# Feed-forward attention: projected rows stay in PSUM through bias and rope; GpSimd makes the whole low part of the later weight pieces

## What is computed

```python
h = _rms_norm(x, ln1_w)                       # 256 selected rows, 512 wide
q = (h @ wq + bq).reshape(S, N_HEADS, HEAD_DIM)      # 16 heads of 128
kk = (h @ wk + bk).reshape(S, N_KV_HEADS, HEAD_DIM)  # 8
v = (h @ wv + bv).reshape(S, N_KV_HEADS, HEAD_DIM)
q = q * cos + _rotate_half(q) * sin
kk = kk * cos + _rotate_half(kk) * sin
...
att = jnp.einsum('shd,thd->hst', q, kk) / np.sqrt(HEAD_DIM)   # causal, softmax
attn_out = jnp.einsum('hst,thd->shd', att, v).reshape(S, N_HEADS * HEAD_DIM) @ wo
x1 = x + attn_out
mlp = jax.nn.silu(h2 @ w_gate) * (h2 @ w_up) @ w_down
```

## Time and profile before

| | us |
|---|---|
| median of 3 timed runs | 909.02 (906.36 to 913.1) |
| span of the profiled execution | 901.1 |
| TensorE busy in it | 826.7 |
| VectorE busy | 622.7 |
| ScalarE busy | 474.8 |
| GpSimd busy | 453.8 |

### The profile page before, as it was taken

One profiled execution on the slowest core, in us unless ns is written; L12 is line 12 of the kernel. 1 busy time (PEld: TensorE's weight loads), 2 busy tenths in 40 slices (PEclk: granted clock), 3 DMA queues, 4 the chain that ended last, 5 costly groups with the idle time before them and its releaser, 6 DMA issues. The chain is left out here.

```text
span 901.1 us, 14347 instructions
## 1 busy us (share of the span) xinstructions
PE 826.7 (92%) x4216; PEld 688.0 (76%) x4216; DVE 622.7 (69%) x1053; ACT 474.8 (53%) x1620; POOL 453.8 (50%) x501
## 2 busy tenths in 40 slices
PE   6999958999999999999999999999977677767997
PEld 5888747888888888888888888888755566656886
DVE  4454445777778777777777777777767988873932
ACT  4556435665565656655655665566552434443441
POOL 2333343555564565555565555565574664442660
PEclk9999989999999999999999999999998988999999
DMA  6656553111111111111112112110156342213520
GB/s 202 205 188 219 176 177 129 26 58 58 35 47 58 35 47 58 35 47 58 45 37 70 35 35 70 47 44 27 45 171 224 133 148 73 85 47 117 187 94 23
DMA packets 49288, 81.38 MB, mean 90 GB/s; under 512 B 4144, under 2 KB 12464, under 8 KB 49264
## 3 DMA queue, kind: packets, MB, share of 16 engines
q1 hardware_dynamic: 48688, 79.25, 26.9%
q0 software_dynamic: 576, 1.84, 0.6%
HBM read 63.77 MB, written 17.30 MB: 90 GB/s over the span
## 5 line engine op out<-in xcount | busy, mean ns | idle before, releaser
L1026 ACT ACTIVATE sq_junk<-q_row 128x128 bf16<-128x128 f32 x256 | 76.1, 298 | 157.6 <-DVE q_row L1280 157.6
L1034 ACT ACTIVATE p_row<-s_row,neg_max 128x128 f32<-128x128 f32 x256 | 99.8, 391 | 37.5 <-DVE neg_max L1301 37.5
L1689 PE MATMUL b_y<-wo_hi,oT_hi 128*128 128x512 f32 x256 | 106.8, 417 | 1.0 <-DVE oT_lo L1211 1.0
L1689 PE MATMUL b_q<-wq_hi,xT_hi 128*128 128x512 f32 x252 | 105.4, 418 | 2.2 <-DVE k_row L1234 2.2
L1690 PE MATMUL b_y<-wo_lo,oT_hi 128*128 128x512 f32 x256 | 101.0, 394 | 0.0
L1691 PE MATMUL b_y<-wo_hi,oT_lo 128*128 128x512 f32 x256 | 100.8, 394 | 0.0
L764 POOL TENSOR_TENSOR p_row<-p_row,p_inv 128x512 f32<-128x512 f32 x64 | 66.6, 1040 | 67.1 <-DVE p_inv L1310 67.1
L1691 PE MATMUL b_q<-wq_hi,xT_lo 128*128 128x512 f32 x252 | 99.6, 395 | 0.0
L1690 PE MATMUL b_q<-wq_lo,xT_hi 128*128 128x512 f32 x252 | 99.2, 393 | 0.0
L722 POOL TENSOR_TENSOR q_rs<-q_ss,eps_head 128x4 f32<-128x4 f32 x64 | 12.8, 199 | 151.4 <-ACT sq_junk L1026 151.4
L832 POOL TENSOR_TENSOR wp_lo<-raw,wp_hi 128x1024 fp32r<-128x1024 f32 x24 | 71.5, 2986 | 30.8 <-ACT wp_hi L938 30.8
(11 more groups left out here) (287 smaller groups left out, 2352.7 us busy)
## 6 DMA issues: line engine op xcount, KB each, us to landing
cx<-in_ctx_dram SPq DMA_DIRECT2D x16, 256.0 KB, 2.7
wq_raw<-in_L_xattn_Wq_dram SPq DMA_DIRECT2D x16, 256.0 KB, 2.7
wo_raw<-in_L_xattn_Wo_dram SPq DMA_DIRECT2D x16, 256.0 KB, 3.1
v_store<-v_out SPq DMA_DIRECT2D x16, 256.0 KB, 3.3
k_store<-k_out SPq DMA_DIRECT2D x16, 256.0 KB, 2.1
xr<-in_x_dram SPq DMA_DIRECT2D x16, 256.0 KB, 2.7
k_raw<-k_store SPq DMA_DIRECT2D x16, 256.0 KB, 2.6
v_raw<-v_store SPq DMA_DIRECT2D x16, 256.0 KB, 2.8
```

What stands on the lines that cost most here:

```text
L1026: sq = act.activation(sq_junk[:, h, :], q_row[:, h, :], ACT.Square, accum_out=q_ss[:, h:h + 1])
L1034: e = act.activation(p_row[:, h, :], s_row[:, h, :], ACT.Exp, bias=neg_max[:, h:h + 1], accum_out=p_sum[:, h:h + 1])
L1689: pe.matmul(dst, left[0], right[0], start=start, stop=False)
```

## The change

- The bias is added in place in PSUM; `proj` is no longer used here (it still is in the MLP). The sines are read from PSUM, the cosine product is made in place in PSUM on VectorE, and the addition reads PSUM and `by_sin`. GpSimd has no part in the rope.
- The value tiles' high part is copied from PSUM, and VectorE makes the low part, from PSUM (`value_low`).
- A bank is free for the next tile only when the tile is roped or its value-low part is made (`wait_bank_read`). The first eight tiles rotate over three banks, with b_s2 as the third; the others over two.
- Of pieces 4 to 23 GpSimd makes all four rows of the low part; of pieces 0 to 3 each engine still makes half.
- VectorE's order: each tile is finished in one go, and the weight-low parts from piece 4 on are gone from it.

The diff without its unchanged lines:

```diff
@@ -301,6 +301,7 @@
+        early_proj = [b_q, b_y, b_s2]
@@ -478,6 +479,21 @@
+        def bank_of(r):
+            return early_proj[r % 3] if r < AHEAD * NJ else f_proj[r % 2]
+        def values(o, j):
+            return NJ * PROJECTIONS[o][1] + j
+        def wait_bank_read(eng, r):
+            before = [k for k in range(r) if bank_of(k) is bank_of(r)]
+            if before:
+                o, j = TILES[before[-1]]
+                if PROJECTIONS[o][0] == "v":
+                    eng.wait_ge(fv_lo_done, values(o, j) + 1)
+                else:
+                    eng.wait_ge(f_roped, ROPED.index((o, j)) + 1)
@@ -634,7 +650,7 @@
-                    sp.wait_ge(piece_lo_dve, RAW_BEFORE[n] + 1)
+                    sp.wait_ge(piece_lo_dve, min(RAW_BEFORE[n] + 1, NSLOT))
@@ -829,8 +845,9 @@
-                pool.tensor_tensor(wp_lo[n % NSLOT][:, 0:2, :], raw[RAW_OF[n]][:, 0:2, :],
-                                   wp_hi[n % NSLOT][:, 0:2, :].bitcast(fp32),
+                part = slice(0, 2 if n < NSLOT else 4)
+                pool.tensor_tensor(wp_lo[n % NSLOT][:, part, :], raw[RAW_OF[n]][:, part, :],
+                                   wp_hi[n % NSLOT][:, part, :].bitcast(fp32),
@@ -849,55 +866,17 @@
-            def by_cosine(o, j):
-                r, k = TILES.index((o, j)), ROPED.index((o, j))
-                pool.wait_ge(f_biased, r + 1)
-                pool.wait_ge(gathered_rope[j], 16)
-                wait(pool, f_roped, k)
-                pool.tensor_tensor(by_cos[:].rearrange("p (h d) -> p h d", h=QUAD),
-                                   proj[r % 2][:].rearrange("p (h d) -> p h d", h=QUAD),
-                                   rope[j][:, 0:HD].unsqueeze(1).to_broadcast([P, QUAD, HD]),
-                                   ALU.mult).then_inc(cos_done, 1)
-            def v_low_rows(r, i):
-                pool.wait_ge(fv_hi_done, i + 1)
-                c = i // NJ
-                pool.tensor_tensor(fv_lo[:, i % NJ, c * W:(c + 1) * W], proj[r % 2][:],
-                                   fv_hi[:, i % NJ, c * W:(c + 1) * W].bitcast(fp32),
-                                   ALU.subtract).then_inc(fv_lo_done, 1)
-            def take_rows(o, j):
-                kind, n = PROJECTIONS[o]
-                if kind == "v":
-                    v_low_rows(TILES.index((o, j)), NJ * n + j)
-                else:
-                    by_cosine(o, j)
-            take_rows(0, 0)
-            take_rows(1, 0)
-            take_rows(2, 0)
-            take_rows(3, 0)
-            for o in range(AHEAD):
-                take_rows(o, 1)
-                if o > 0:
-                    split_low(NSLOT + o - 1)
-            def next_query_cosine(n, j):
-                by_cosine(PROJECTIONS.index(("q", n + 1)), j)
+            for o in range(1, AHEAD):
+                split_low(NSLOT + o - 1)
-                    next_query_cosine(n, 0)
-                    next_query_cosine(n, 1)
@@ -908,9 +887,6 @@
-                if n == 0:
-                    for j in range(NJ):
-                        take_rows(PROJECTIONS.index(("v", 1)), j)
@@ -1109,7 +1085,7 @@
-                copy(fv_hi[:, j, n * W:(n + 1) * W], proj[TILES.index((o, j)) % 2][:]).then_inc(fv_hi_done, 1)
+                copy(fv_hi[:, j, n * W:(n + 1) * W], bank_of(TILES.index((o, j)))[:]).then_inc(fv_hi_done, 1)
@@ -1487,12 +1463,12 @@
-                dve.tensor_tensor(proj[r % 2][:], f_proj[r % 2][:], bias_row[u % 2][:],
+                dve.tensor_tensor(bank_of(r)[:], bank_of(r)[:], bias_row[u % 2][:],
-                q = proj[r % 2][:].rearrange("p (h a d) -> p h a d", h=QUAD, a=2)
+                q = bank_of(r)[:].rearrange("p (h a d) -> p h a d", h=QUAD, a=2)
@@ -1502,10 +1478,12 @@
-            def add_rotated(k, j):
-                dve.wait_ge(cos_done, k + 1)
+                q = bank_of(r)[:].rearrange("p (h d) -> p h d", h=QUAD)
+                dve.tensor_tensor(q, q, rope[j][:, 0:HD].unsqueeze(1).to_broadcast([P, QUAD, HD]),
+                                  ALU.mult).then_inc(cos_done, 1)
+            def add_rotated(r, k, j):
@@ -1514,7 +1492,14 @@
-                dve.tensor_tensor(turned[j][:], by_cos[:], by_sin[:], ALU.add).then_inc(f_roped, 1)
+                dve.wait_ge(cos_done, k + 1)
+                dve.tensor_tensor(turned[j][:], bank_of(r)[:], by_sin[:], ALU.add).then_inc(f_roped, 1)
+            def value_low(o, j):
+                n = PROJECTIONS[o][1]
+                dve.wait_ge(fv_hi_done, values(o, j) + 1)
+                low(fv_lo[:, j, n * W:(n + 1) * W], bank_of(TILES.index((o, j)))[:],
+                    fv_hi[:, j, n * W:(n + 1) * W]).then_inc(fv_lo_done, 1)
@@ -1525,44 +1510,35 @@
-                if r >= 2 and PROJECTIONS[TILES[r - 2][0]][0] == "v":
-                    before, block_ = TILES[r - 2]
-                    dve.wait_ge(fv_hi_done, NJ * PROJECTIONS[before][1] + block_ + 1)
-                    dve.wait_ge(fv_lo_done, NJ * PROJECTIONS[before][1] + block_ + 1)
-                    rotate(r, ROPED.index((o, j)), j)
-            def finish_rows(o, j):
-                if PROJECTIONS[o][0] != "v":
-                    add_rotated(ROPED.index((o, j)), j)
+                    k = ROPED.index((o, j))
+                    rotate(r, k, j)
+                    add_rotated(r, k, j)
-            finish_rows(0, 0)
+            fk_low(0, 0)
+            value_low(1, 0)
-            fk_low(0, 0)
-            finish_rows(2, 0)
-            finish_rows(3, 0)
-            for o in range(AHEAD):
-                take_rows(o, 1)
-                if o > 0 and PROJECTIONS[o - 1][0] == "k":
-                    fk_low(PROJECTIONS[o - 1][1], 1)
-                finish_rows(o, 1)
-                if o > 0:
-                    split_low(NSLOT + o - 1)
+            take_rows(0, 1)
+            take_rows(1, 1)
+            fk_low(0, 1)
+            value_low(1, 1)
+            take_rows(2, 1)
+            take_rows(3, 1)
+            fk_low(1, 1)
@@ -1593,13 +1569,9 @@
-                    finish_rows(o, 0)
-                    finish_rows(o, 1)
-                if 0 < n < FQ - 1:
-                    split_low(split_early(n))
@@ -1617,23 +1589,21 @@
-                    split_low(split_early(n))
-                for piece in split_late(n):
-                    split_low(piece)
+                if n == 0:
+                    for j in range(NJ):
+                        value_low(PROJECTIONS.index(("v", 1)), j)
-            split_low(split_early(FQ - 1))
-            split_low(P_MLP + 2)
@@ -1645,7 +1615,6 @@
-            split_low(P_MLP + 3)
@@ -1661,8 +1630,6 @@
-                for piece in split_mlp(m):
-                    split_low(piece)
@@ -1883,7 +1850,8 @@
-                pe.wait_ge(piece_lo_dve, n + 1)
+                if n < NSLOT:
+                    pe.wait_ge(piece_lo_dve, n + 1)
@@ -1906,8 +1874,8 @@
-                wait(pe, f_biased, r - 1)
-                project(f_proj[r % 2], j, ATTENTION.index(PROJECTIONS[o])).then_inc(f_projected, 1)
+                wait_bank_read(pe, r)
+                project(bank_of(r), j, ATTENTION.index(PROJECTIONS[o])).then_inc(f_projected, 1)
```

## The result

| | before | after |
|---|---|---|
| median of the timed runs, us | 908.98 (906.36 to 913.1, 4 runs) | 877.14 (876.61 to 879.73, 4 runs) |
| span of the profiled execution | 901.1 | 878.0 |
| TensorE busy in it | 826.7 | 820.9 |
| VectorE / GpSimd busy | 622.7 / 453.8 | 577.5 / 464.0 |

The ratio after to before is 0.9669, with a 95% interval of 0.9637 to 0.9701: 31.8 us less. Forecast were 880, within 873 to 894.

A forecast was written before the change was run, and what follows sets the result against it. VectorE's waits for GpSimd were taken to leave TensorE 42 us idle in the feed-forward attention. Net gains of 29.2 from 901.1 gave 871.9 profiled; with 7.9 outside the span the forecast was 880 us, range 873 to 894.

The forecast's parts named there:

- A tile at 3.0: Each projected key or query tile, bias to rope addition on VectorE: 3.0 us instead of 7.6 for a quarter's second tile.
- The dear-write rival: VectorE's bias and cosine writes to PSUM cost 1.29 each, a tile takes 4.2, total 892 us; chance 0.12.
- A piece at 4.65: GpSimd making the whole low part of one weight piece takes 4.65 us undisturbed; upper bound 6.9.
- Quarters 12.6, 20.4, 19.2: Feed-forward attention, quarters 0, 1, 2: these lengths in us, gains 4.3, 10.8, 6.1; TensorE becomes the middle quarters' bound.
- Start-up, gain 8.3: Layer 2's first tile to the first query turn: tiles at 3.0 without weight-lows between them gain 8.3 us.
- Quarter 3, one cold stretch of 1.7: Quarter 3, without projection: TensorE idles of 2.3 and 1.9 us bring one stretch at 1.2 GHz, charged 1.7 us.
- TensorE's idle from 42 to about 14: Feed-forward attention: VectorE stops waiting for GpSimd, so TensorE's idle falls from 42 to about 14 us; chance 0.68.
- The signs: Changed profile if right: by_sin 0.41, weight-low 4.6 to 4.8, middle quarters 19 to 21, first MLP tile near 796.
- The norm 1.1 late: Behind the output product: GpSimd's longer piece 14 delays the row norm and everything behind it by 1.1 us.
- The gating row: Before the MLP: a small VectorE instruction may wait 4.6 us for GpSimd, holding the first gating row 1 us.
- 7.9 us outside the span: The median timed run is 7.9 us above the profiled span, for starting and ending outside it.
- GpSimd becomes the bound: At 6.9 us a piece, scalings slip in quarters 1 and 2, norm and MLP lose too: 894 us; chance 0.12.

The follow-up runs named there:

- after again: The changed kernel with nothing altered, run once more as a reference on the same chip; measured 878.0, ratio 0.9659 to the kernel before.
- the third: The changed kernel with nothing altered, run a third time as reference for three reorderings; measured 877.58, ratio 0.9672 to the kernel before.

## Why the prediction was right, point by point

The mechanism, the side and the size of the whole were right; the table's row "forecast" shows which terms were. From layer 2's first tile to the MLP's it adds up to 129.6 us, and 130.2, 128.5 and 129.2 were measured. That agreement is in part luck: the start-up came out 2.0 to 3.9 longer, the stages of quarter 3 and before the MLP together 2.9 shorter. (The gains in the prediction go by the stages of this table, 16.9, 31.2 and 25.3; rows 2 has them rounded.)

- *A tile at 3.0.* Measured 3.06. Bias in place takes 689 to 700 ns, the cosine read and written in PSUM 699 to 700, a sine 411 to 425. The dear-write rival is refuted. The Trainium skill (VectorE: DVE Perf Modes, the section on the TRN2 errata) charges 62 cycles more for a PSUM source than for an SBUF source. That does not show: the addition with an input in PSUM takes 691 to 694, and the same addition reading SBUF, in the kernel with the bias in SBUF, takes 691 to 693 where GpSimd does not hold it.
- *A piece at 4.65.* The groups give a mean of 4.63 for 20 pieces of 2048. The wait in the median of 3.09 was for VectorE's half, as argued.
- *Quarters 12.6, 20.4, 19.2.* Measured 12.5, 20.2 and 19.2, three times over. The reading "TensorE becomes the bound" was only half of it: with VectorE 1.2 dearer a tile each of these stages grew by the full 2.4 to 2.8. They are a chain through both engines, which the hand-offs of the schedule held and the sums of busy time did not.
- *Start-up, gain 8.3.* Measured 4.4, and 5.4 and 6.2 in the other two executions. The mis-sized term of the sum. The second block's first tile was to start 22.3 behind the first (690.0) and started 24.9, 24.9 and 23.7 behind it. I took the first sines to wait for nobody, which is true, but VectorE's weight-low ahead of them does (two SBUF inputs): 1.2. And the tile behind the second block's rows starts at 1.2 GHz (695.41, 0.79): 14 matmuls at a spacing of 0.43 instead of 0.23 in after, 10 in after again, 7 in the third. By these spacings that is 2.8, 2.0 and 1.5, where I charged nothing (the kernel before has such a stretch there too, 7 to 8 matmuls from 692.58 on). From that tile to the query turn the forecast had 17.6 and 18.9, 18.2 and 17.8 were measured; with the excess of the slow matmuls taken off that is 16.1 to 16.3, so the forecast had 1.3 to spare there, and priced the chain up to the tile 1.4 too short besides the 1.2.
- *Quarter 3, one cold stretch of 1.7.* It did not come: the idles there are 1.67 and 1.74 and behind both the matmuls start at 0.50 and 0.30. The stage took 20.7 instead of 21.9. A second one, charged before the MLP, came 4 us later, behind the MLP's first tile (0.77 at 800.73): to the MLP 13.9 instead of 15.6, the MLP 77.3 instead of 74.7.
- *TensorE's idle from 42 to about 14.* It went to 22. The prediction took the whole gain off the idle; a third of it came off the busy time, by fewer matmuls at the lower clock.
- *The signs.* Sines, rope rows and middle quarters came as listed. The pieces were 4.58 to 5.01, the longest over the 4.8. The MLP's first tile came at 800.7, 799.0 and 796.9, not near 796 each time, and TensorE was not unbroken from there: the gating row below stopped it. Of the signs against the forecast one showed, and small: the last transposes of probabilities were released by GpSimd's scalings, 0.84 us at 783.55.
- *The norm 1.1 late.* Confirmed: in the kernel with the norm first the stage is 12.8, 1.1 less.
- *The gating row.* It waited 4.60 for GpSimd, as said. I had laid its 1 us inside an idle that was there anyway; it made one of its own, 0.85 before 814.65. VectorE's row of after, and GpSimd's of the norm, which follows a piece as before:

```profile
809.12 4.60 DVE L1619 TENSOR_SCALAR g_one<-g_exp 128x2 f32<-128x2 f32 x1 [2.17 <-ACT g_exp L1166]
```

```profile
796.39 0.19 POOL L855 TENSOR_SCALAR f_ms<-f_ss 128x1 f32<-128x1 f32 x1
```

- *7.9 us outside the span.* Wrong. Each timed run of all these kernels is 1.7 to 1.9 longer than its own span. The spans of before go from 902.0 (clock 0.973) to 911.5 (0.960) in later runs; the execution in rows 1 to 7, with 901.1, lies below them all. So the forecast of 880 is near 877 by two errors that cancel: 6.1 too little in the span, 6.2 too much around it. Of the 6.1, 2.8 lie in the later start of layer 2, behind code that did not change, and 2.6 in the MLP; 0.6 lie in the stages that the change touches. The gain between the medians is 31 to 32, that of the profiles 23.1, 23.8 and 26.7. The kernel before has more long idles behind which the clock can fall, and its time scatters more; I did not test which of them make the difference between that execution and its median, so where the last 4 to 9 us of the gain arise stays open.
- *GpSimd becomes the bound*, 0.12. It did not, but the margin was thinner than the price I gave it (14 instead of 29 at 7.0 a piece). Of that 14, 4.6 for the MLP has no working in the prediction, and by its own numbers (an estimate) nine pieces of 6.9 against eleven of 5.6 leave 0.5; the MLP lost 6.5.

## What to carry to other kernels

Before moving work between VectorE and GpSimd, list VectorE's instructions with two SBUF inputs that can meet GpSimd's, since each waits for the end of the GpSimd instruction (the small TENSOR_SCALAR with one SBUF input did, too, 4.60 us, while a TENSOR_REDUCE with one did not the earlier trace rows); a longer GpSimd instruction makes that dearer (+11 us here), and putting one operand in PSUM takes it away (43 us here). Two halves of such a change must be judged together. Against a sum, hold stage lengths of several executions, not one profile, and check the part outside the span run by run.

## What was not expected of the hardware

- Which of two engines holds the port is decided by 0.05 us or less, and costs the later one up to the whole of the other's instruction; two executions of one kernel differ by 1.2 us there.
- VectorE's in-place bias and cosine in PSUM cost about 10 ns more than rows that write SBUF: the bias has a median of 700 in b_q and 691 in b_y against 686 and 677 before, the cosine 699 against 692 in the kernel with the bias in SBUF.
- One place of one kernel gave 14, 10 and 7 matmuls at 1.2 GHz in three executions, behind idles of 2.28, 2.93 and 2.47 us: the length of idle does not say how long the stretch is. The Trainium skill (TensorE: Matmul & The Clock Gate, "Part 1: The HAM clock gate") calls this number variable from run to run, and the three executions agree.
